# GNN layer in fp32 halves: GpSimd normalises the second batch, and the first batch's hand-written order is changed

## The reference

```python
h = maximum(layernorm(x, axis=-1), 0.0)                  # eps 1e-5
A = stack([adj, adj, shifted, adj.T, adj.T, shifted.T, eye])   # 7 relations
HW = einsum('bnf,rfo->rbno', h, W[:, :F]) + einsum('rd,rdo->ro', W_edges, W[:, F:])[:, None, None, :]
out = x + max(einsum('rbnm,rbmo->rbno', A, HW), axis=0) + b
```

## Time and profile before

| | |
|---|---|
| median of 3 runs | 223.4 us (222.56 to 223.49) |
| the profiled execution | 223.7 us, its span 221.7 us |
| TensorE matmuls busy | 211.5 us (95%), 1069 |
| VectorE busy | 179.2 us (81%), 388 |
| ScalarE busy | 186.0 us (84%), 468 |
| GpSimd busy | 163.8 us (74%), 179 |
| DMA | 38.71 MB, mean 175 GB/s |
| TensorE's granted clock, mean | 0.994 of full |

### The profile page before, as it was taken

The page is one execution under the profiler, slowest core; times in us unless marked ns, Lnnn a source line. Parts: engine busy times, 40 slices in busy tenths (PEclk is TensorE's granted clock), DMA queues, the critical chain, the costliest instruction groups (busy, mean ns, idle before and its releaser), DMA issues.

```text
span 221.7 us, 4960 instructions
## 1 busy us (share of the span) xinstructions
PE 211.5 (95%) x1069; PEld 174.5 (79%) x1069; DVE 179.2 (81%) x388; ACT 186.0 (84%) x468; POOL 163.8 (74%) x179
## 2 busy tenths in 40 slices
PE   7898999999999999999999999999999999999980
PEld 5777678887888888888888888888888888887760
DVE  3795799796989879797887969887887969777683
ACT  3767999998998989898898989899898989887640
POOL 1370499979596996969697896969699696969241
PEclk9999999999999999999999999999999999999997
DMA  5928976959596986768596877758597776236725
GB/s 178 302 91 184 243 199 171 263 113 252 135 248 143 245 180 157 231 158 215 122 254 145 198 206 155 235 136 218 131 230 190 165 222 146 43 53 143 158 37 89
DMA packets 91152, 38.71 MB, mean 175 GB/s; under 512 B 71575, under 2 KB 80903, under 8 KB 91143
## 3 DMA queue, kind: packets, MB, share of 16 engines
q1 hardware_dynamic: 90055, 38.48, 70.3%
q10 hardware_dynamic: 1088, 0.13, 0.4%
HBM read 34.33 MB, written 4.26 MB: 174 GB/s over the span
## 4 chain that ended last, share of the span: by engine, by line
PE 85%; DVE 6%; ACT 2%; DMA 2%; issue 2%; SPq 0%; DVEq 0%; ACTq 0%
PE at_ps L745 11%; PE rel_ps L765 11%; PE rel_ps L767 11%; PE rel_ps L766 11%; PE bwd_ps L765 6%; PE bwd_ps L767 6%; PE bwd_ps L766 6%; PE fwd_ps L765 6%; PE fwd_ps L767 6%; PE fwd_ps L766 6%; PE turn_ps L753 3%; DMA a_sb<-in_adj 2%; DVE h_lo L692 1%; DVE best L595 1%; PE rel_ps L762 1%
## 5 line engine op out<-in xcount | busy, mean ns | idle before, releaser
L304 POOL TENSOR_TENSOR a_lo<-a_sb,a_hi 128x512 fp32r<-128x512 f32 x62 | 79.1, 1298 | 37.8 <-ACT a_hi L386 37.8
L595 DVE TENSOR_TENSOR best<-rel_ps,best 128x512 f32<-128x512 f32 x62 | 42.6, 687 | 13.7 <-PE rel_ps L767 13.6
L566 DVE TENSOR_TENSOR at_lo<-at_ps,at_hi 128x512 fp32r<-128x512 f32 x62 | 41.2, 685 | 8.2 <-ACT at_hi L394 7.6
L434 ACT ACTIVATE rel_ps<-sum_all,c_col 128x512 f32<-128x512 f32 (+1 forms) x63 | 41.8, 679 | 4.5 <-DVE best L595 2.9
L386 ACT ACTIVATE a_hi<-a_sb 128x512 fp32r<-128x512 f32 x64 | 39.4, 617 | 3.8 <-DMA a_sb<-in_adj 3.8
L394 ACT ACTIVATE at_hi<-at_ps 128x512 fp32r<-128x512 f32 x62 | 36.3, 590 | 6.5 <-PE at_ps L745 6.3
L745 PEld LDWEIGHTS at_ps<-ident,a_sb 128*128 128x128 f32 x240 | 28.1, 141 | 4.2
L745 PE MATMUL at_ps<-ident,a_sb 128*128 128x128 f32 x240 | 31.2, 272 | 0.0
L592 DVE SCALAR_TENSOR_TENSOR best<-rel_ps,c_col,best 128x512 f32<-128x512 f32 x32 | 23.9, 747 | 6.9 <-PE rel_ps L767 5.8
L319 POOL TENSOR_TENSOR xb_sb<-xp_sb,bias_sb 128x512 f32<-128x512 f32 x16 | 22.7, 1421 | 5.9 <-DMA xp_sb<-in_x 5.9
L765 PE MATMUL bwd_ps<-a_hi,h_hi 128*128 128x512 f32 x64 | 27.0, 421 | 0.0
(11 more groups left out here) (103 smaller groups left out, 438.9 us busy)
## 6 DMA issues: line engine op xcount, KB each, us to landing
a_sb<-in_adj SPq DMA_DIRECT2D x64, 256.0 KB, 3.3
sum_all<-sums_dram SPq DMA_DIRECT2D x16, 512.0 KB, 4.1
x_sb<-in_x SPq DMA_DIRECT2D x16, 256.0 KB, 3.7
xp_sb<-in_x SPq DMA_DIRECT2D x64, 64.0 KB, 3.6
out<-o_sb SPq DMA_DIRECT2D x60, 64.0 KB, 2.0
w_sb<-in_L_gnn_W SPq DMA_DIRECT2D x1, 448.0 KB, 6.0
sums_dram<-sum_rows SPq DMA_DIRECT2D x16, 4.0 KB
bias_sb<-in_L_gnn_b SPq DMA_DIRECT2D x4, 64.0 KB, 2.2
```

What stands on the lines that cost most here:

```text
L304: pool.tensor_tensor(a_lo[q][:, j, :], a_sb[q][:, j, :], a_hi[q][:, j, :].bitcast(fp32), ALU.subtract).then_inc(a_lo_ready[j], 1)
L434: act.activation(to[:, cols], sum_all[q][:, 0 if r in FWD else 1, cols], ACT.Copy, scale=c_col[:, r:r + 1]).then_inc(after_it, 1)
L566: dve.tensor_tensor(at_lo[q][:, i, :], at_bank(b, i)[:], at_hi[q][:, i, :].bitcast(fp32), ALU.subtract).then_inc(at_lo_ready[i], 1)
L595: dve.tensor_tensor(best[q][:], held[:], best[q][:], ALU.max).then_inc(joined[r], 1)
```

## The change

GpSimd gets `normalise_second`: for batch 1 it writes max(x - mean, 0) piece by piece (four tensor_scalar instructions on 128x128, with the mean's column as scalar), then multiplies each piece by its column of `rstd` (four more), and raises `h_ready`. This equals the relu of the normalised value, as rstd is positive. ScalarE no longer normalises batch 1. ScalarE's, VectorE's and TensorE's `first_step` are put in another order, the constants' matmul goes to `turn_ps`, and TensorE's wait for `c_ready` stands ahead of turn_h rather than of the first relation.

```diff
--- before.py
+++ after.py
@@ -128,6 +128,7 @@
 
         bn_done, mean_var_ready, ve_ready, rstd_ready, shift_ready = (
             sem(s) for s in ("bn_done", "mean_var_ready", "ve_ready", "rstd_ready", "shift_ready"))
+        centred = sem("centred")
         h_ready, h_hi_ready, h_lo_ready = sem("h_ready"), sem("h_hi_ready"), sem("h_lo_ready")
         h_turned, ht_hi_ready, ht_lo_ready = sem("h_turned"), sem("ht_hi_ready"), sem("ht_lo_ready")
         a_hi_ready = [sem(f"a_hi_ready{j}") for j in range(C)]
@@ -325,6 +326,17 @@
                 wait(pool, out_stored[q], G * 16 * k)
                 pool.tensor_tensor(o_sb[q][:], turned[q][:], xb_sb[q][:], ALU.add).then_inc(out_ready, 1)
 
+            def normalise_second():
+
+                for j in range(C):
+                    pool.tensor_scalar(h_sb[1][:, j, :], x_sb[1][:, j, :], mean_var[1][:, j, 0:1], 0.0,
+                                       op0=ALU.subtract, op1=ALU.max).then_inc(centred, 1)
+                for j in range(C):
+                    pool.wait_ge(centred, j + 1)
+                    last = pool.tensor_scalar(h_sb[1][:, j, :], h_sb[1][:, j, :], rstd[1][:, j:j + 1], None,
+                                              op0=ALU.mult)
+                last.then_inc(h_ready, 1)
+
             def first_step():
                 ahead = (0, 1)
                 split_a(0, 0, 2)
@@ -333,6 +345,7 @@
                 pool.wait_ge(w_hi_ready, 1)
                 pool.tensor_tensor(w_lo[:, W_DVE:, :], w_sb[:, W_DVE:, :], w_hi[:, W_DVE:, :].bitcast(fp32),
                                    ALU.subtract).then_inc(w_lo_ready, 1)
+                normalise_second()
 
             def step(k, q, left):
                 if is_batch(2 * k + q, 1):
@@ -449,15 +462,14 @@
                 take_sums(0, 0)
                 round_at(*ahead, 0)
                 round_at(*ahead, 1)
-                normalise(*ahead)
+                round_a(*ahead, 0)
+                round_a(*ahead, 1)
+                round_fwd(0, 0)
                 act.wait_ge(c_ready, 1)
                 join_first(0, 0)
-                round_fwd(0, 0)
-                round_ht(*ahead)
                 round_at(*ahead, 2)
                 round_at(*ahead, 3)
-                round_a(*ahead, 0)
-                round_a(*ahead, 1)
+                round_ht(*ahead)
 
             def step(k, q, left):
                 b = 2 * k + q
@@ -613,14 +625,14 @@
                 split_at(*ahead, 0)
                 split_at(*ahead, 1)
                 dve.wait_ge(c_multiplied, 1)
-                dve.tensor_copy(c_col[:], rel_ps[0][:, 0:R]).then_inc(c_ready, 1)
+                dve.tensor_copy(c_col[:], turn_ps[:, 0:R]).then_inc(c_ready, 1)
+                split_fwd(0, 0)
                 round_h(*ahead)
                 dve.wait_ge(h_hi_ready, 2)
                 dve.tensor_tensor(h_lo[1][:], h_sb[1][:], h_hi[1][:].bitcast(fp32),
                                   ALU.subtract).then_inc(h_lo_ready, 1)
-                split_fwd(0, 0)
+                split_at(*ahead, 2)
                 split_ht(*ahead)
-                split_at(*ahead, 2)
                 join(0, 0, EYE[1])
                 join(0, 0, EYE[2])
                 moments(1, 0)
@@ -840,22 +852,23 @@
                 bwd(0, 0, 3)
                 turn_sums(0, 0)
                 turn_a(*ahead, 0)
+                turn_a(*ahead, 1)
                 fwd(0, 0, 1)
                 fwd(0, 0, 2)
-                turn_a(*ahead, 1)
-                fwd(0, 0, 3)
                 pe.wait_ge(we_loaded, 16)
                 pe.wait_ge(wedge_cols_ready, 1)
-                pe.matmul(rel_ps[0][:, 0:R], we_sb[:], wedge_cols[:], start=True, stop=True).then_inc(c_multiplied, 1)
+                pe.wait_ge(ht_lo_ready, 1)
+                pe.matmul(turn_ps[:, 0:R], we_sb[:], wedge_cols[:], start=True, stop=True).then_inc(c_multiplied, 1)
+                fwd(0, 0, 3)
                 pe.wait_ge(w_hi_ready, 1)
                 pe.wait_ge(w_lo_ready, 2)
-                pe.wait_ge(c_ready, 1)
                 eye(0, 0, EYE[0])
-                eye(0, 0, EYE[1])
-                turn_h(*ahead)
-                eye(0, 0, EYE[2])
                 turn_a(*ahead, 2)
                 turn_a(*ahead, 3)
+                pe.wait_ge(c_ready, 1)
+                turn_h(*ahead)
+                eye(0, 0, EYE[1])
+                eye(0, 0, EYE[2])
 
             def step(k, q, left):
                 b = 2 * k + q
```

## The result

The changed kernel takes 224.43 us (median of 11 runs, 223.78 to 225.08) against 223.39 for the kernel before (11 runs, 222.56 to 224.07): ratio 1.0053, 95% interval 1.0034 to 1.0072. It is 0.5% slower, where 0.7 us were forecast to be gained; the time lies inside the range given (to 224.5), on the other side of no change.

A forecast was written before the change was run, and what follows sets the result against it. The kernel was taken as bound by the order of TensorE's work: waits of 0.91 + 0.50 + 0.35 us removed, 1.06 new at turn_h of batch 2, so 0.7 us gained, 222.7 against 223.4; range 221.7 to 224.5.

The forecast's parts named there:

- part 2: GpSimd normalises batch 1: eight 128x128 instructions at 0.37 us each, h ready at 18.3, ahead of TensorE's demand at 19.40.
- the two near rows: Profile rows used to price GpSimd's instructions: affine select of 128x128 at 0.29 us, two-input subtraction at 0.44 for 128x128.
- X: Time at which GpSimd has h of batch 1 ready: 15.38 + 8 x 0.37 = 18.3.
- Rival (a): GpSimd is late with h: nothing gained at X = 19.6, 1.1 us lost at 20.7 (0.67 per instruction); chance 0.17.
- the far row: GpSimd's power of 128x4 at 1.02 us, the farthest price: eight would take 8.2 us, h at 23.5, kernel 227.
- Part 1: TensorE's new order: first relation at 17.87 instead of 18.77, h asked for at 19.40, second step 0.9 us earlier.
- The 0.91 us: TensorE's stand ending at 18.77, ahead of the first relation of h, waiting for c_ready; forecast to be removed.
- Part 3: VectorE's cast of h waits for GpSimd's whole a_lo (1.28 us); joins end at 23.5, and TensorE's 0.50 us wait goes.
- Part 4: x of batch 2 lands at 24.15 and holds moments; turn_h of batch 2 at 29.0, TensorE standing 1.1 us.
- Rival (c): Gain taken elsewhere: a of batch 2 lands late or another hand-over is delayed; 0 to 0.3 us gained; chance 0.13.
- rival (b): Load of x does not cap the gain: 1.4 up to 1.76 us gained, 221.7 to 222.0; chance 0.25.
- The stand of 0.35 us: TensorE's wait ahead of turn_h of batch 2, from 29.37 to 29.72 in the kernel before; counted as removed.

The follow-up runs named there:

- the experiment: Changed kernel with a wait on GpSimd, so its a_lo of batch 1 piece 0 starts only after VectorE's cast of h: 223.70 us, ratio 1.0011.
- ScalarE's kernel: Changed kernel's order on all engines, but ScalarE normalises batch 1 again: 222.32 us, ratio 0.9956; measured again 222.56 us, ratio 0.9955.
- the early loads: New order with ScalarE normalising, plus SP's reloads of x and a for batch 2 ahead of the sums' trip: 221.71 us; again 222.23 us.

## Why the prediction was wrong

**The step that failed** is the price in part 2, "I take 0.37, midway between the two near rows of this size, as one- and two-input forms bracket an instruction with one tensor and one or two columns of scalars". They do not bracket it. The two-tensor bound was right by itself (0.44, measured 0.46), but it lies below all tensor_scalar forms, not above them: 0.71 and 0.60 in the kernel, to which 0.3 for the one that VectorE held (foreseen as "up to 0.4 later", but left out of X) is to be added. X was 20.8 instead of 18.3, which removed the gain and more.

**Rival (a) was what happened**, with its own formula: at 0.67 per instruction h comes at 20.7 and 1.1 us are lost, 224.5; measured 0.67 and 224.43. It had a chance of 0.17. That the time agrees to 0.1 us is partly luck: by the formula moments start at 25.9, and they started at 25.67 in the same count (25.27 and 0.40), because the cast was held 1.07 us and not 1.28; the rest of the loss came a step later, at ScalarE's fill, which the prediction did not have. The prediction named the far row (1.02) as a bound and gave the stretch from 0.44 to it little weight, though nothing in the trace excluded it. The row that looked like the nearest relative by name and size, the affine select at 0.29, reads one tensor, and no form that was priced came down to it; but leaning on it did not turn the sign by itself: 0.44, the dearer of the two near rows, gave X = 18.9, where the gain was still whole. Both near rows were forms other than the one to be priced.

**The estimate from the Trainium skill** (GPSIMD Engine Reference, "Performance pitfalls for Q7 kernels") of 0.085 us for each small read agrees with what a column cost here, 0.07 to 0.09. That a column is read by such a command is not shown. By itself it would have put h at 19.0 and left the sign as it was: columns were the smaller part of what was missing.

**Part 1 held.** The 0.91 us went, c_col was ready in time, TensorE asked for h when forecast (4.79 us behind the transpose of the sums against 4.88). With h in time the second step starts 6.72 us behind it (20.65 less 13.93, ScalarE normalising) instead of 7.65: the 0.9 us forecast. The new order alone gives -0.4%.

**Part 3 held in its mechanism.** The cast was held nearly as long as a_lo ran: 1.28 us forecast, 1.07 measured. With h at 18.3 most of that would have fallen into time in which VectorE had other work, and the 0.3 us left over were written off as of no use to anyone. With h at 20.4 VectorE had already stood 1.48 us, so that the whole 1.07 came onto the path, and the joins, not x, ended last. The rule of the Trainium skill (SBUF — State Buffer, "Who interferes with whom") agrees both ways: a 1.50 us cast behind a_lo, and in the experiment a 1.80 us a_lo behind h_lo.

**Part 4 was right in some executions.** In the changed kernel x of batch 2 is not waited for. With h early it is, 0.67 and 0.88 us in two traces, and moments started at the landing; in a third they were not held. Rival (c) named the landing of a as another such wait, and it was seen too (1.06 us). Both come and go with the execution, as rival (b) had allowed. With h in time the forecast of 0.7 us is about what comes: 1.05 (223.37 less 222.32) and 0.75 (223.31 less 222.56) in the two measurements of ScalarE's kernel. But these are medians over executions with and without the cap, from no gain to two us, and so no test of the sum. Where neither landing is waited for, with the early loads, turn_h of batch 2 is 1.6 us ahead of the kernel before and the median of 221.71 is the one that rival (b) gave, 221.7 to 222.0; measured again it was 222.23. The stand of 0.35 us ahead of turn_h is still there in that trace (27.61 less 26.47 less 0.79), as moments are ahead by the same 1.6 (8.75 us behind the transpose of the sums instead of 10.34).

## What to carry to other kernels

When an operation goes to an engine where no row prices its form, put its price into the range up to the far row and ask first how much lateness the sum bears; here 0.16 us more for each of eight instructions would have used the gain up, 0.30 more came, and a few lines on scratch in an idle stretch price it. A producer that is late by a little is doubly dear if its engine's next instruction blocks the consumer: order the consumer's cast ahead of it. Removing one wait on TensorE in a hand-ordered start can pay only up to the next landing, so look at when the loads for the stretch behind are issued, and at more than one trace: here two executions of one kernel were 2.4 us apart, one with these waits and one without.

## What the runs showed of the hardware

On GpSimd a tensor_scalar on 128x128 fp32 took 0.53 us in its plainest form (one operation, a constant) and 0.73 with two operations and a column, against 0.46 for a subtraction of two tensors of the same size, which reads twice as much. VectorE's fp32 cast of 128x512 took 0.43 alone and 1.50 when it was issued 0.07 us behind the start of a GpSimd subtraction of 1.27. The holding works the other way too: a subtraction on GpSimd took 1.80 instead of 1.27 beside VectorE's h_lo, and a tensor_scalar 1.03 instead of 0.71 beside its w_lo. TensorE, after a stand of 1.63 us and one of 0.26, was granted half its clock for about 3 us, and its matmuls took 0.63 instead of 0.40.
